# A deformable convolution block: sampling in chunks of 512 pixels, and fusion of the sampled maps by row sums

## The reference

```python
out_normal = conv(x, w_normal)
offset = concat([conv(x, w_offx), conv(x, w_offy)])      # 18 channels: dy, dx of 9 taps
out_x = deform_conv(x, offset, w_dx)                     # bilinear samples of x at the shifted places,
out_y = deform_conv(x, offset, w_dy)                     # then a product over channels and taps
out = conv(concat([out_normal, out_x, out_y]), w_fusion) # 384 -> 128 channels
out = relu(bn(out, bn1))
out = bn(conv(out, w_conv2), bn2)
return relu(out + x)
```

## Time and profile before

| | |
|---|---|
| Median of 3 runs | 2706.13 us (2704.74 to 2708.22) |
| Profiled execution: its time | 2708.34 us |
| Profiled execution: span of the trace | 2706.5 us |
| TensorE (PE), VectorE (DVE), ScalarE (ACT), GpSimd (POOL) busy | 2607.4, 1845.0, 2002.0, 1906.5 us |
| Gathers | 1800, 471.97 MB |
| Mean granted TensorE clock | 0.984 of 2.4 GHz |

### The profile page before, as it was taken

One profiled execution on the slowest core, in us unless ns is written; L12 is line 12 of the kernel. 1 busy time (PEld: TensorE's weight loads), 2 busy tenths in 40 slices (PEclk: granted clock), 3 DMA queues, 4 the chain that ended last, 5 costly groups with the idle time before them and its releaser, 6 DMA issues.

```text
span 2706.5 us, 51420 instructions
## 1 busy us (share of the span) xinstructions
PE 2607.4 (96%) x17840; PEld 2598.7 (96%) x17840; DVE 1845.0 (68%) x4940; ACT 2002.0 (74%) x4925; POOL 1906.5 (70%) x1806
## 2 busy tenths in 40 slices
PE   3679999999999999999999999999999999999999
PEld 3679999999999999999999999999999999999999
DVE  5777677676677677777766776776766676777730
ACT  5677777777777777777777777777777777777741
POOL 6777777777777777777777777777777777677720
PEclk7789999999999999999999999999999999999999
DMA  5766776667676667766676766666667676676620
GB/s 171 217 207 192 211 206 203 200 192 210 197 206 199 200 203 207 202 200 203 200 203 200 203 196 204 201 197 194 205 193 209 196 206 199 202 207 194 195 76 20
DMA packets 162404, 522.70 MB, mean 193 GB/s; under 512 B 30944, under 2 KB 31072, under 8 KB 161760
## 3 DMA queue, kind: packets, MB, share of 16 engines
q0 software_dynamic: 144000, 471.97, 60.6%
q1 hardware_dynamic: 18144, 47.44, 5.0%
HBM read 506.18 MB, written 13.11 MB: 192 GB/s over the span
## 4 chain that ended last, share of the span: by engine, by line
PE 91%; DVE 3%; ACT 2%; DMA 2%; issue 1%; POOL 1%; ACTq 0%; POOLq 0%; DVEq 0%
PE work L341 19%; PE work L347 19%; PE work L344 19%; PE acc L344 7%; PE acc L341 7%; PE acc L347 7%; PE turned L373 7%; PE work L326 4%; DMA cells<-in_cells,index 2%; POOL cells L300 1%; DVE mixed L678 1%; PE work L333 1%; ACT mixed L473 0%; ACT samp L473 0%; DVE samp L684 0%
## 5 line engine op out<-in xcount | busy, mean ns | idle before, releaser
L300 POOL DMA_INDIRECT cells<-in_cells,index x1800 | 1895.2, 1053 | 684.5 <-issue 335.3
L473 ACT ACTIVATE mixed<-cells,wgt 128x256 f32<-128x256 f32 x1800 | 761.7, 499 | 53.7 <-DMA cells<-in_cells,index 53.0
L473 ACT ACTIVATE samp<-mixed,wgt 128x128 f32<-128x128 f32 x1800 | 620.6, 396 | 205.0 <-DVE mixed L678 196.5
L678 DVE SCALAR_TENSOR_TENSOR mixed<-cells,wgt,mixed 128x256 f32<-128x256 f32 x1800 | 746.6, 480 | 31.6 <-ACT mixed L473 30.1
L341 PE MATMUL work<-feat,w_hi 128*128 128x320 f32 x2160 | 691.3, 320 | 1.4 <-ACT off_c L472 1.4
L347 PE MATMUL work<-feat,w_lo 128*128 128x320 f32 x2160 | 676.0, 313 | 0.0
L344 PE MATMUL work<-feat,w_hi 128*128 128x320 f32 x2160 | 675.7, 313 | 0.0
L684 DVE SCALAR_TENSOR_TENSOR samp<-mixed,wgt,samp 128x128 f32<-128x128 f32 x1800 | 513.6, 348 | 59.3 <-ACT samp L473 59.3
L637 DVE TENSOR_TENSOR samp_lo<-turned,samp_hi 128x640 fp32r<-128x640 f32 x360 | 295.7, 821 | 274.8 <-ACT samp_hi L472 274.8
L341 PE MATMUL acc<-samp_hi,w_hi 128*128 128x320 f32 x1440 | 449.0, 312 | 0.0
L344 PE MATMUL acc<-samp_lo,w_hi 128*128 128x320 f32 x1440 | 447.6, 311 | 0.0
(11 more groups left out here) (70 smaller groups left out, 3182.7 us busy)
## 6 DMA issues: line engine op xcount, KB each, us to landing
cells<-in_cells,index POOLq DMA_INDIRECT x1800, 3.7
x_raw<-in_xflat SPq DMA_DIRECT2D x40, 410.0 KB, 4.1
late<-in_x SPq DMA_DIRECT2D x40, 320.0 KB, 5.4
out<-late SPq DMA_DIRECT2D x40, 320.0 KB, 3.7
late<-in_weights SPq DMA_DIRECT2D x3, 1152.0 KB, 7.6
cells<-in_weights SPq DMA_DIRECT2D x1, 657.0 KB, 4.0
cst<-in_const SPq DMA_DIRECT2D x1, 199.0 KB, 4.9
bnp<-in_bn SPq DMA_DIRECT2D x1, 4.0 KB, 4.6
```

What stands on the lines that cost most here:

```text
L300: eng.indirect_dma_start(out=cells[:, g, :], out_offset=None, in_=table[0:(b + 1) * CELLS, :], in_offset=bass.IndirectOffsetOnAxis(ap=inde ...
L473: return eng.activation(dst, src, ACT.Copy, scale=scale)
L678: eng.scalar_tensor_tensor(out=mixed[:, tp, j], in0=cells[:, (k * TILES + j) % GSLOTS, 2 * C:4 * C], scalar=wgt[:, par, 1, 0, j, k:k + 1], ...
```

## The change

1. **Chunks.** Sampling no longer goes by strips but by chunks of 512 flat pixels, 50 chunks of nine taps (450 slots), four tiles each. A slot of the program is one tap of one chunk. The ring of gathered tiles has 10 slots. A step (one strip) has 11 or 12 slots.
2. **Partial products in PSUM.** ScalarE writes its products to `part_m` (two banks, used by pairs of tiles) and `part_s` (one bank); VectorE adds from there and writes `mixed`. `deform_tap` has six products of 512 pixels, into one bank for each map.
3. **Fusion.** The normal map keeps its nine products (E), for even and odd rows. For the two sampled maps sums and differences of neighbouring rows are formed (`map_sums`, high and low parts by `map_high` and `map_low`), and the weights' rows are combined likewise once at the start; four groups G0 to G3 of six products then give two output rows each. VectorE adds the groups into `y_even` and `y_odd` with factors 1, 0.5, -0.5 and -1 (`fused_add`), onto E copied there by ScalarE (`fused_start`).
4. **Even slices.** The products of a step are listed in `ORDER` and cut evenly over its slots, and the two work banks are handed out in turn in the order in which groups first appear.

The diff, cut to its core:

```diff
+GSLOTS = 10
+PACE_LAG = 5 * CT + 1
+MIXED = 3
+STEPS = NS + 3
+DELAY = 1
+ORDER = [("N", 0, 0, 9), ("N", 1, 0, 9), ("E", 0, 0, 9), ("E", 1, 0, 3), ("O", 0, 0, 3), ("E", 1, 3, 9), ("C", 0, 0, 3),
+         ("O", 1, 0, 3), ("C", 0, 3, 9), ("C", 1, 0, 3), ("T", 0, 0, 1), ("C", 1, 3, 9),
+         ("G", 3, 0, 6), ("G", 1, 0, 6), ("G", 2, 0, 6), ("G", 0, 0, 6)]
+TRIPLES = sum(b - a for _, _, a, b in ORDER)
+LEADS = {"O": 2, "T": 2, "N": 1, "E": 0, "C": -3}
+LAST_SLOT = 1 + DELAY + (45 * STEPS) // 4
+def first_slot(i):
+    return DELAY + (45 * i) // 4
+BANK = {}
+for _g in [("O", 0, 0), ("O", 1, 0), ("T", 0, 0), ("N", 0, 0), ("N", 1, 0)] + [_s[:3] for _l in SLICES for _s in _l]:
+    BANK.setdefault(_g, len(BANK) % 2)
...
         @block.tensor
+            def take(bank, signal, value):
+                at_least(eng, *reader[bank])
+                reader[bank] = (signal, value)
...
+                    take(bank, *{"N": (n_lo_done, 2 * s + part + 1), "E": (e_out, 2 * s + part + 1),
+                                 "C": (c_out, 2 * s + part + 1),
+                                 "G": (even_step if part == 0 else odd_step, 3 * s + (3 if part == 0 else part))}[job])
...
+            for T in range(LAST_SLOT):
+                if T + 1 < NT:
+                    turn_samples(T + 1)
+                for job, part, s, a, b in SLICES[T]:
+                    if job == "O":
+                        offsets(s, part, a, b)
+                    elif job == "T":
+                        turn_offsets(s)
+                    else:
+                        group(job, part, s, a, b)
+                if T < NT:
+                    deform_tap(T)
...
         @block.scalar
+                    copy(part_m[:, j // 2, j % 2], cells[:, n % GSLOTS, 0:2 * C],
+                         scale=wgt[:, 0, 0, t, k:k + 1]).then_inc(part_m_done, 1)
...
+            for T in range(LAST_SLOT):
+                sample_part(T + 2)
+                samples_high(T + 1)
+                if T % TAPS == 0 and 0 < T <= NT:
+                    maps_out(T // TAPS - 1)
+                mixed_part(T + 3)
+                if T in WEIGHTS_AT:
+                    weights_high(WEIGHTS_AT[T])
+                for stage_v in (0, 1):
+                    if T - 1 - stage_v in V_AT:
+                        map_high(V_AT[T - 1 - stage_v], stage_v)
+                for job, part, s in done(T - 1):
+                    if job == "G" and part in (0, 3):
+                        middle_edge(s, part // 3)
+                for job, part, s in done(T):
+                    if job == "O":
+                        off_evac(s, part)
+                    elif job == "N":
+                        normal_out(s, part)
+                    elif job == "E":
+                        fused_start(s, part)
+                    elif job == "C":
+                        result(s, part)
+                    elif job == "T":
+                        turned_evac(s)
+                    elif part in (0, 3):
+                        middle(s, part // 3)
+                if T in X_AT:
+                    x_high(X_AT[T])
...
         @block.vector
+                    eng.scalar_tensor_tensor(
+                        out=mixed[:, T % MIXED, j], in0=cells[:, n % GSLOTS, 2 * C:4 * C],
+                        scalar=wgt[:, 1, 0, t, k:k + 1], in1=part_m[:, j // 2, j % 2], op0=ALU.mult, op1=ALU.add,
                     ).then_inc(mixed_done, 1)
...
+            def fused_add(s, m):
+                eng.wait_ge(g_done[m], s + 1)
+                got = work[BANK["G", m, s]][:, 0:HALF]
+                ye, yo = y_even[:, s % 2], y_odd[:, s % YODD]
...
+            for T in range(LAST_SLOT):
+                sample(T + 2)
+                samples_low(T + 1)
+                mix(T + 3)
+                if T in WEIGHTS_AT:
+                    weights_low(WEIGHTS_AT[T])
+                for job, part, s in done(T - 1):
+                    if job == "G" and part in (0, 3):
+                        middle_low(s, part // 3)
+                for job, part, s in done(T):
+                    if job == "N":
+                        normal_low(s, part)
+                    elif job == "C":
+                        residual(s, part)
+                    elif job == "G":
+                        fused_add(s, part)
+                    elif job == "T":
+                        indices(s)
+                if T in X_AT:
+                    x_low(X_AT[T])
+                for stage_v in (0, 1):
+                    if T - 1 - stage_v in V_AT:
+                        map_low(V_AT[T - 1 - stage_v], stage_v)
+                    if T - stage_v in V_AT:
+                        map_sums(V_AT[T - stage_v], stage_v)
```

More of the change, by code:

```diff
@@ L89, with slot_done, last_chunk @@
+def slot_done(job, part, s):
+    return next(T for T in range(LAST_SLOT) if (job, part, s) in done(T))
+def last_chunk(s):
+    return ((s + 1) * PIX + CHUNK - 1) // CHUNK - 1
+V_AT = {}
+for _s in range(NS):
+    _t = TAPS * last_chunk(_s) + TAPS
+    V_AT[max(_t, slot_done("G", 0, _s - 1) + 1) if _s else _t] = _s
+assert len(V_AT) == NS
 BN_STEPS = 9
 NIDX = 10
-NCONST = 128 + 2 * TILES * TAPS + 4 * (STEPS + 1)
-class Flags:
-    def __init__(self, i=None):
-        mid = i is None
-        self.strip = mid or i < NS
-        self.nxt = mid or i + 1 < NS
-        self.load = mid or i + 2 < NS
-        self.top = mid or 1 <= i < NS
-        self.bot = mid or 1 <= i <= NS
-        self.fuse = mid or 2 <= i < NS + 2
-        self.mtop = mid or 3 <= i < NS + 2
-        self.mbot = mid or 3 <= i <= NS + 2
-        self.resid = mid or 3 <= i < NS + 3
-        self.second = mid or 4 <= i < NS + 4
-        first = not mid and i < FIRST_STEPS
-        self.slices = FIRST_SLICES if first else SLICES
-        self.done = done(self.slices)
-        self.turn = 2 if first else 3
-        self.weights = {} if mid else WEIGHTS_AT.get(i, {})
-    def has(self, job):
-        return {"O": self.nxt, "F": self.fuse, "N": self.strip, "C": self.second}[job]
@@ L120, in run_steps, with deform_block @@
-def run_steps(eng, step):
-    for i in range(STEPS):
-        step(i, i % 2, Flags(i))
+NCONST = 128 + 2 * PER + 4 * (NS + 1)
 def at_least(eng, sem, value):
-    if isinstance(value, int) and value <= 0:
+    if value <= 0:
         return
     eng.wait_ge(sem, value)
-def deform_block(nc, x, xflat, table, weights, bn, const, out):
+def deform_block(nc, x, xflat, corners, weights, bn, const, out):
     ctx = ExitStack()
@@ new lines, in fused_start, with middle @@
+            def fused_start(s, part):
+                eng.wait_ge(e_done, 2 * s + part + 1)
+                if s == 0 and part == 0:
+                    eng.wait_ge(w_lo_done, 4)
+                at_least(eng, mid_lo_done, 2 * (s - 3) + 2 if part else 2 * (s - 2) + 1)
+                y = y_odd[:, s % YODD] if part else y_even[:, s % 2]
+                copy(y, work[BANK["E", part, s]][:, 0:HALF]).then_inc(e_out, 1)
+            def middle(s, odd):
+                par, n = s % 2, 2 * s + odd
+                rows = even_rows(1 + odd)
+                at_least(eng, c_done, 2 * (s - 2) + 2)
+                if odd:
+                    eng.wait_ge(odd_step, 3 * s + 3)
+                else:
+                    eng.wait_ge(even_step, 3 * s + 3)
+                y = y_odd[:, s % YODD] if odd else y_even[:, s % 2]
+                eng.activation(y, y, ACT.Relu, bias=scale1[:, 1:2], scale=scale1[:, 0:1]).then_inc(mid_f_done, 1)
+                eng.wait_ge(mid_f_done, n + 1)
+                copy(mid[:, par, 0, rows, 1:1 + W], rows2(y)).then_inc(mid_hi_done, 1)
@@ new lines, in middle_low, with residual @@
+            def middle_low(s, odd):
+                par, rows = s % 2, even_rows(1 + odd)
+                eng.wait_ge(mid_hi_done, 2 * s + odd + 1)
+                y = y_odd[:, s % YODD] if odd else y_even[:, s % 2]
+                low(mid[:, par, 1, rows, 1:1 + W], rows2(y), mid[:, par, 0, rows, 1:1 + W]).then_inc(mid_lo_done, 1)
+            def residual(s, half):
+                eng.wait_ge(c_done, 2 * s + half + 1)
+                if half == 0:
+                    eng.wait_ge(resid_in, 16 * s + 16)
+                part = resid[:, half * HALF:(half + 1) * HALF]
+                eng.scalar_tensor_tensor(out=part, in0=work[BANK["C", half, s]][:, 0:HALF], scalar=scale1[:, 2:3],
+                                         in1=part, op0=ALU.mult, op1=ALU.add).then_inc(c_out, 1)
@@ L708, in _ @@
             weights_low(0)
[L709 removed]
+            x_low(0)
             eng.wait_ge(bn_in, 16)
```

852 lines of the change are left out of this document (441 added, 411 removed), and 9 rows, old and new, of the table SLICES.

## The result

The changed kernel takes 3020.7 us (median; 3016.15 to 3022.08), the kernel before 2705.4 on the same terms: a ratio of 1.116, 95% interval 1.1141 to 1.118. The forecast was 2880 us in a range of 2690 to 3000. The direction and the place of the loss were right, and the time lies above the range. The profiled execution has a span of 3017.9 us (its run 3019.8).

What follows compares the result with a forecast made beforehand. The prediction took TensorE's own work, 64.47 us a strip, to bound the kernel before, and bank waits to slow the changed one. It summed 45 + 184 + 2600 + 51 = 2880 us, range 2690 to 3000.

Steps and rivals of the forecast that it cites:

- What bounds the kernel now: Steady strips of the kernel before: TensorE's own work sets the 64.47 us a strip, and it waits for nobody.
- what is taken off TensorE: TensorE's work per strip: fewer fusion matmuls and longer sampled products bring 64.47 down to 58.8 us, 5.2 a slot.
- What is added to the other engines: Partial products, map sums and accumulations: ScalarE some 55 and VectorE 56 us a strip, no price for PSUM.
- rival 2: ScalarE's 256 products much quicker into PSUM: decides from 0.29 us each, about 2660 us at 0.25 without lateness; chance 0.13.
- rival 5: VectorE's sums with a PSUM operand cost 0.05 us more each, the walk ending near 3060 us; chance 0.02.
- The three bank waits: TensorE waits for banks, C0 on E1, C1 on C0, G3 on C1: at least 2.6, 1.9, 2.3 us in 11 slots.
- the walk: One 11-slot step followed engine by engine: waits 4.5, 2.6, 2.5 and 1.8 us, ending at 69.7, 6.34 us a slot.
- the least waits: TensorE's waits without built-up lateness: 7.9 us a strip at the least, making a strip 66.7 us.
- Rivals 1 and 3: 1: engines on time, least waits, 2747 us, chance 0.18. 3: waits don't arise, gather paces, 2521 us, chance 0.08.
- The 6.25 us a slot: Pace of the 416 later slots: the middle of the walk's 6.34 and 6.17 with shorter ScalarE writes, 2600 us.
- the sum: Whole kernel: 45 us to the first slot, 184 for 34 early slots, 2600 for 416 slots, 51 at the end: 2880.
- Rival 4: Clock falls to half speed in TensorE's waits, two a strip: 160 us more, 3040; sign, granted clock under 0.95; chance 0.05.

Runs made afterwards that it cites:

- e8_decoupled: e1_banks with ScalarE's result, middle, middle_edge and middle_low moved one or two slots later, so it no longer waits for VectorE at slot end: 2677.0 us.
- e1_banks: The changed kernel with only the bank order altered: an interrupting group takes the other bank, the next new group the interrupting one's: 2813.5 us.
- e9_all: e8_decoupled with O1 and T slipped in three products later, input copies a slot earlier, and map sums ahead of VectorE's accumulations and index chain: 2663.9 us.
- e2_filler: The changed kernel with 10, 9 and 10 unread products put on TensorE ahead of C0, C1 and G3: 2975.0 us.
- e10_no_vsum: e9_all without its moved map sums, so e8_decoupled plus later O1 and T and earlier input copies: 2681.5 us.

## Why the prediction was wrong, point by point

**What bounds the kernel, and what is taken off TensorE: right.** The 36 matmuls and the longer sampled products are as counted: the step of 512 columns came to 0.232, between the 0.226 taken and the bound of 0.234. `e8_decoupled` has 241.75 us of busy time in four strips against the 235.2 of the count, with a clock of 0.98.

**What is added to the other engines: nearly right.** VectorE has 52.5 us of work a strip and ScalarE 50.6, where 56 and 55 were said. Neither rival about PSUM holds. For rival 2, ScalarE's product into PSUM would have had to come to 0.29 us by the prediction; redone with its own terms, (2706 - 280) / 416 x 11.25 = 65.6 us a strip and not 65.1, it is 0.33. It takes 0.415 in a row of four. The Trainium skill ("ScalarE: Activation LUTs", "Step-by-step: what each stage is for") has PSUM as the faster destination. The trace agrees for the single product, a mean of 466 ns into PSUM and of 499 into SBUF; back to back, which is what counts here, it shows a gain of 0.005 us. For rival 5, the sums of 256 and of 128 take the same 0.41 and 0.28 us as with both operands in SBUF. The Trainium skill ("VectorE: DVE Perf Modes", the section on the TRN2 errata) has a larger fixed cost for a PSUM source; these rows speak against it.

**Where TensorE waits: right in place, somewhat too long in size.** The three bank waits are there as named, at 4.04, 1.79 and 2.29 us in the strip shown, where the walk had 4.5, 2.6 and 2.5. TensorE's busy share fell to the 85% given. Idle time in four strips is 41.06 us, 10.3 a strip; the walked step had 11.4 in its four waits. That they are not on time was right too: the least waits would have been 7.9, and `e8_decoupled`, where idle time fell from the 26.4 us of `e1_banks` to 15.5, shows that much of the lateness comes from the two engines waiting for each other. Rivals 1 and 3 needed waits shorter than that or none.

**The step that failed: the clock.** The 6.25 us a slot were 5.2 of work and 1.05 of waits. The 6.60 of the steady slots are 5.23 of work, 0.91 of waits (41.06 / 45) and 0.46 (20.6 / 45) of busy time beyond the work, of which 0.31 (14 / 45) are steps at the lower clock. That term stands at nothing in the sum. Rival 4 had it, at 160 us and 3040 us in all, and its sign, a granted clock under 0.95, came: 0.934 over the span. For 416 slots the four strips shown give 14 x 416 / 45 = 129 us; the 28 strips from 428.58 to 2508.61, with 35.9 us of busy time at the lower level in every four, give 146. So its price was about right, and its chance, 0.05, was wrong, and with it the upper end of the range. The waits, 0.14 us a slot shorter than in the sum, took back a part of the error.

The fault was in reading: from two idle times, 3.24 us with transposes at 0.74 and 3.88 us with transposes at 1.30, the prediction took a bound between the two, below which a wait costs only its own length. But the reading stopped at the transposes. In the same trace the products behind the 3.24 us run at half speed from 85.54 on, 1.1 us after the transposes began, and those behind a wait of 2.24 us do so too (0.47 long for 0.31), though no other wait of over 1 us lies in the 26 us before it:

```profile
85.54 0.47 PE L341 MATMUL acc<-samp_hi,w_hi 128*128 128x320 f32 x1
...
204.17 0.74 PE L373 MATMUL turned<-cst,samp 128*128 128x128 f32 x5 [2.24 <-DVE samp_lo L637]
...
204.89 0.47 PE L344 MATMUL work<-feat,w_hi 128*128 128x320 f32 x1
```

So the kernel before already showed that waits of the length that the prediction forecast can cost half speed. In the steady part of the changed kernel half-speed steps follow a wait of 1.79 us, when a wait of 4.04 lies 10 us before it, and none follow one of 2.29 that comes later. A wait's own length doesn't decide alone: half speed came behind 2.24 us in the one kernel and not behind 2.29 in the other. The cost of several such waits a strip should have been bounded from nothing to all products behind them at half speed.

**The other terms.** The second turn, the start of the first slot, came at 42.0 us (45 said), that of the 35th slot at 248.9, so 207 us for 34 slots where 184 were said, with 45.6 us of idle time and a clock of 0.89 in that stretch. The last sampled product ended at 2962.0 and the span 56 us later (51 said). The 416 slots between took 2713 us, 6.52 each, where 2600 were said. Of the 138 us between the span and the sum, 113 lie there, 20 in the early slots and 5 at the end.

```profile
42.00 1.12 PE L436 MATMUL turned<-cst,mixed 128*128 128x128 f32 x4 [2.97 <-DVE mixed L762]
...
248.88 0.60 PE L436 MATMUL turned<-cst,mixed 128*128 128x128 f32 x4
```

**What stays open.** How much idle time, how close together, makes the clock fall isn't settled by these runs. And `e8_decoupled` and `e9_all` still have some 16 us of idle time in four strips, the largest part of it ahead of the products that need the map's low part (6.7 and 6.4 us).

## What to carry to other kernels

When a change takes work from the engine that sets the pace, ask first who empties its banks, and in what place of the other engines' order: a bank handed to the next group in line makes every late copy a stall, and of the 315 us lost here 207 came back by an order of the banks alone and 136 more, past the kernel before, by letting two engines not wait for each other inside a slot. A stall of TensorE costs more than its length, because products behind it can run at half speed: a forecast with several waits of 2 to 4 us in a short time needs a term for the clock. An engine's share of busy time says little when four engines are within 10% of each other; here the order of their work alone was worth more than the whole loss, with the work the same.

## What the runs showed of the hardware

- The granted clock fell to the lower level (steps of 0.27 us for 0.150) behind waits of 4.04 and 1.79 us 10 us apart, and stayed at 1.00 behind one of 2.29 us. In the kernel before it fell behind waits of 3.24 and 2.24 us. The mean over the four strips went from 1.00 to 0.94 in the changed kernel, and back to 0.98 where either the waits were filled (`e2_filler`) or taken away (`e1_banks`, `e8_decoupled`). The Trainium skill ("TensorE: Matmul & The Clock Gate", "A second HAM failure mode: psum-queue depth-cycling") tells of a kernel whose short idle times between groups that cycle through PSUM banks make the clock go up and down; this trace agrees, with 0.66 and 0.81 in pieces of 6 us around the bank waits.
- More work made a kernel faster: 116 unread products in four strips (17.4 us) shortened them by 9.2 us.
- With the same idle time, one wait of TensorE (6.44 us) in place of two (4.49 and 2.12) went with faster steps: 6.4 for 11.4 us of busy time at the lower level in four strips (`e9_all` against `e10_no_vsum`).
- ScalarE writes 256 elements a partition to PSUM and to SBUF at the same pace in a row (0.415 and 0.42 us), though a single product is shorter into PSUM (a mean of 466 ns for 499), and VectorE reads an operand from either at the same cost (0.41 us each in a row).
